# Reordering the hand-over from attention to the feed-forward stage: GpSimd takes the first row scalings

## The reference, cut to what matters

```python
x = x + cross_attention(layernorm(x), ctx_4096, Wq, bq, Wk, bk)
x = x + latent_attention(layernorm(x), ..., Wo)      # 128 heads of 8 + 64 rotary columns; out @ Wo
x = x + ffn(layernorm(x), W1, b1, W2, b2)

def _linear8bit(x, W, b):                             # ffn is two of these: 1024 -> 4096 -> 1024
    col_max = jnp.max(jnp.abs(x), axis=rows)
    outlier = col_max > 3.0
    x_in, x_out = jnp.where(outlier, 0.0, x), jnp.where(outlier, x, 0.0)
    y = quant_rows(x_in) @ quant_rows(W).T            # each row: round(a / s) * s, s = max|a| / 127
    return y + x_out @ W.T + b
```

## Time and profile before

| | |
|---|---|
| median of 3 runs | 964.59 us (961.07 to 964.97) |
| profiled execution, its own time | 964.59 us |
| its span, first to last instruction | 962.6 us |
| TensorE matmul busy | 899.3 us (93%) |
| DVE busy | 732.3 us (76%) |
| ACT busy | 607.4 us (63%) |
| GpSimd busy | 480.5 us (50%) |
| mean granted TensorE clock | 0.980 |

### The profile page before, as it was taken

The page is one execution under the profiler, slowest core; times in us unless marked ns, Lnnn a source line. Parts: engine busy times, 40 slices in busy tenths (PEclk is TensorE's granted clock), DMA queues, the critical chain, the costliest instruction groups (busy, mean ns, idle before and its releaser), DMA issues.

```text
span 962.6 us, 18936 instructions
## 1 busy us (share of the span) xinstructions
PE 899.3 (93%) x6809; PEld 821.2 (85%) x6809; DVE 732.3 (76%) x1140; ACT 607.4 (63%) x1050; POOL 480.5 (50%) x314
## 2 busy tenths in 40 slices
PE   5999999999997899999999999998779999799996
PEld 5997888888886789999999998886679999699996
DVE  6456666677446468889999998876978889899964
ACT  4424344565525478888887878782778787466652
POOL 0220000244427697767667676662176676176682
PEclk9999999999998999999999999999799999799999
DMA  7566675777663778655665655544053442224221
GB/s 276 222 221 219 266 269 213 283 303 274 259 189 100 227 241 260 188 174 176 186 195 166 194 159 172 193 164 187 15 175 104 159 165 97 88 89 176 87 88 44
DMA packets 80007, 174.81 MB, mean 182 GB/s; under 512 B 7584, under 2 KB 57536, under 8 KB 77376
## 3 DMA queue, kind: packets, MB, share of 16 engines
q1 hardware_dynamic: 79376, 173.76, 52.5%
q10 hardware_dynamic: 560, 0.09, 0.1%
HBM read 161.51 MB, written 11.53 MB: 180 GB/s over the span
## 4 chain that ended last, share of the span: by engine, by line
PE 28%; POOL 13%; issue 12%; DVE 7%; ACT 4%; DMA 1%; POOLq 0%; SPq 0%; DVEq 0%; ACTq 0%
POOL W_all L2121 8%; PE bank L51 6%; PE bank L52 6%; PE bank L53 6%; POOL W_all L1802 4%; PE bank L1268 3%; PE bank L1297 3%; PE bank L1298 2%; PE bank L1313 1%; ACT bank L1429 1%; DVE sx L1122 1%; DVE am L1496 1%; DMA ring<-in_L_attn_Wq_rope_dram 1%; POOL wl L935 1%; DVE nmax L1473 1%
## 5 line engine op out<-in xcount | busy, mean ns | idle before, releaser
L935 POOL TENSOR_TENSOR wl<-ring,wh 128x1024 fp32r<-128x1024 f32 x68 | 161.5, 2394 | 0.0
L51 PE MATMUL bank<-act_all,W_all 128*128 128x256 f32 (+1 forms) x512 | 155.6, 304 | 5.7 <-POOL W_all L1802 2.5
L51 PE MATMUL bank<-act_all,wh 128*128 128x256 f32 x512 | 144.8, 283 | 3.4 <-PEq L940 1.7
L53 PE MATMUL bank<-act_all,W_all 128*128 128x256 f32 (+1 forms) x512 | 145.3, 284 | 0.0
L52 PE MATMUL bank<-act_all,wh 128*128 128x256 f32 x512 | 144.6, 282 | 0.0
L53 PE MATMUL bank<-act_all,wl 128*128 128x256 f32 x512 | 144.0, 281 | 0.0
L457 POOL TENSOR_TENSOR xa_WT_l<-ring,xa_WT_h 128x1024 fp32r<-128x1024 f32 x16 | 43.2, 2720 | 176.8 <-ACT xa_WT_h L452 166.9
L2121 POOL TENSOR_TENSOR W_all<-rnd,W_all 128x512 fp32r<-128x512 f32 x72 | 92.3, 1293 | 59.3 <-ACT W_all L2032 59.2
L932 POOL CAST wh<-ring 128x1024 fp32r<-128x1024 f32 x68 | 68.7, 1040 | 97.7 <-PE bank L53 88.7
L1491 DVE TENSOR_TENSOR pl<-bank,ph 128x512 f16<-128x512 f32 x128 | 88.1, 688 | 32.1 <-ACT ph L1439 29.3
L51 PEld LDWEIGHTS bank<-act_all,W_all 128*128 128x128 f32 x512 | 97.6, 191 | 8.2 <-POOL W_all L1802 3.0
(11 more groups left out here) (259 smaller groups left out, 2613.5 us busy)
## 6 DMA issues: line engine op xcount, KB each, us to landing
ring<-in_ctx_dram SPq DMA_DIRECT2D x16, 2048.0 KB, 7.9
ring<-in_L_attn_Wq_rope_dram SPq DMA_DIRECT2D x32, 1024.0 KB, 6.4
ring<-in_L_ffn_W_dram SPq DMA_DIRECT2D x16, 2048.0 KB, 7.8
panel<-in_L_ffn_W_dram SPq DMA_DIRECT2D x48, 512.0 KB, 4.2
w1p<-in_L_ffn_W_dram SPq DMA_DIRECT2D x16, 512.0 KB, 3.8
ring<-in_L_xattn_Wq_dram SPq DMA_DIRECT2D x2, 2048.0 KB, 11.6
ring<-in_L_xattn_Wk_dram SPq DMA_DIRECT2D x2, 2048.0 KB, 8.4
opv<-stage SPq DMA_DIRECT2D x32, 128.0 KB, 1.7
```

Source lines behind the costliest of these rows:

```text
L51: pe.matmul(out, lh, rh, start=start, stop=False, skip_group_check=True)
L53: return pe.matmul(out, ll, rh, start=False, stop=stop, skip_group_check=True)
L935: pool.tensor_tensor(half_of(l, i), half_of(r, i), f32(half_of(h, i)), ALU.subtract).then_inc(w_lo, 1)
```

## The change

`wo_slots(1, 4, 8)` puts the last slot of `k` = 3 ahead of `attend(31)` on TensorE. On ACT, `ot_high(act, 3)` goes ahead of the two loads. On DVE, `combine(6, 0)` and `combine(6, 1)` go behind the last `low_p`. SP no longer waits for the last outputs to be loaded before it issues the load of block 0 of `W1`. The row scaling of blocks 0 and 1 of `W1` moves from ACT to GpSimd (semaphore `t_first`), as does the scaling of row tile 1 of `onat` from DVE (`ys_pool`). TensorE's first two turns of block 0 move from `y_scaled` to between the two row tiles of `y_turned`, and the turns of block 1 in `first_step` start one product earlier.

```diff
--- before.py
+++ after.py
@@ -1386,9 +1386,8 @@
                     scores_k(g, 2)
                     wo_slots(1, 2, 4)
                     scores_k(g, 3)
-                    wo_slots(1, 4, 7)
+                    wo_slots(1, 4, 8)
                     attend(g)
-                    wo_slots(1, 7, 8)
                     for k in range(4, KT):
                         for q in range(QT):
                             for h in range(2):
@@ -1461,8 +1460,8 @@
                             ot_high(act, OT_AT[g])
                     for k in (6, 7):
                         high_wo(k)
+                    ot_high(act, 3)
                     load_outputs(act, NG - 1, range(2, GROUP))
-                    ot_high(act, 3)
                     ot_high(act, 4)
 
                 def heads_vector(dve, link):
@@ -1520,14 +1519,13 @@
                         low_p(g, 2)
                         if valid(g - 1):
                             stage_outputs(dve, g - 1)
-                        if g == NG - 1:
-                            for op in range(2):
-                                combine(dve, NG // 4 - 2, op)
                         low_p(g, 3)
                         if valid(g) and g % 2 == 1 and g < NG - 1:
                             maximum_w1(LATE + g // 2)
                         if g in OT_AT and g < NG - 2:
                             ot_low(dve, OT_AT[g])
+                    for op in range(2):
+                        combine(dve, NG // 4 - 2, op)
                     stage_outputs(dve, NG - 1)
                     for op in (2, 3):
                         combine(dve, NG // 4 - 2, op)
@@ -1588,7 +1586,7 @@
                 sem(n) for n in ("y3_ready", "q1_chain", "q1_b", "q1_hi", "q1_lo"))
             ln_shift, y_act, y_dve = sem("ln_shift"), sem("y_act"), sem("y_dve")
             y_inl, y_masked, y_masked7, m_ready = (sem(n) for n in ("y_inl", "y_masked", "y_masked7", "m_ready"))
-            ys_act, ys_dve, ys_ready = (sem(n) for n in ("ys_act", "ys_dve", "ys_ready"))
+            ys_act, ys_pool, ys_ready, t_first = (sem(n) for n in ("ys_act", "ys_pool", "ys_ready", "t_first"))
             rowm = sb(ff, "rowm", [P, 2, QT])
             COLS = [slice(h * HALF, (h + 1) * HALF) for h in range(2)]
 
@@ -1883,7 +1881,6 @@
                     heads_sync(sp)
                     sp.wait_ge(w_lo, NW * 2 - 2)
                     sp.wait_ge(wo_pool, 2)
-                    sp.wait_ge(o_loaded[LAST % 2], (LAST // 2 + 1) * 4 * GROUP * 16)
                     load(sp, 0, raw(0), w1_t[0])
                     sp.wait_ge(w_lo, NW * 2)
                     sp.wait_ge(wo_pool, 3)
@@ -1928,6 +1925,11 @@
                                 last = pe.transpose(bank[4 + k // 2][:, c:c + P], onat[:, t, k * P:(k + 1) * P], ident[:, :])
                                 if t == QT - 1 and k % 2:
                                     last.then_inc(y3_ready, 1)
+                            if t == 0:
+                                pe.wait_ge(t_first, CH)
+                                pe.wait_ge(x2_done, 2)
+                                for k in range(EARLY):
+                                    turn(0, 0, k)
 
                     def masked_rows():
 
@@ -1943,16 +1945,13 @@
 
                     def y_scaled():
 
-                        pe.wait_ge(t_ready, CH)
-                        for k in range(EARLY):
-                            turn(0, 0, k)
                         pe.wait_ge(row_factor, 1)
                         for a in (6, 7):
                             pe.matmul(bank[a][:, :], zero[:, 0:P], zero[:, :], start=True, stop=False, skip_group_check=True)
                         for k in range(KT):
                             if k % 4 == 0:
                                 pe.wait_ge(ys_act, k // 4 + 1)
-                                pe.wait_ge(ys_dve, k // 4 + 1)
+                                pe.wait_ge(ys_pool, k // 4 + 1)
                             for t in range(QT):
                                 c = (k % 2) * T + t * P
                                 last = pe.transpose(bank[2 + k // 2][:, c:c + P], onat[:, t, k * P:(k + 1) * P], ident[:, :])
@@ -1981,14 +1980,14 @@
                                 turn(0, 0, 6)
                             elif k == 2:
                                 turn(0, 0, 7)
+                                pe.wait_ge(t_first, 2 * CH)
+                                turn(1, 1, 0)
                             else:
-                                if k == 3:
-                                    pe.wait_ge(t_ready, 2 * CH)
-                                turn(1, 1, k - 3)
+                                turn(1, 1, k - 2)
                             if k == KT - 3:
                                 pe.wait_ge(q1_b, 6)
                                 spread_factors(pe, 0)
-                        for k in range(KT - 3, KT):
+                        for k in (KT - 2, KT - 1):
                             turn(1, 1, k)
                         pe.wait_ge(sx_copied, 1)
 
@@ -2051,6 +2050,7 @@
                                     act.wait_ge(r_max, c * CH - (CH - 1))
                                 biased(c, b, j)
 
+                    act.sem_inc(t_ready, 2 * CH)
                     heads_scalar(act)
                     act.activation(exp_table[:, :], ident[:, 0:1], ACT.Sqrt)
 
@@ -2065,21 +2065,12 @@
                         y_row(0, h)
                     layernorm_root(act, 2, 1)
                     y_row(1, 1)
-
-                    def scale_w1(c, j):
-                        scale_rows(c, USE_W1, j, rw1[:, CH * c + j:CH * c + j + 1])
-
-                    act.wait_ge(q1_chain, 2)
-                    scale_w1(0, 0)
                     for kk in range(KT // 2 - 1):
                         act.wait_ge(y_inl, kk + 1)
                         for i in range(2):
                             k = 2 * kk + i
                             act.activation(ym[:, k, :], bank[4 + kk][:, i * T:(i + 1) * T], ACT.Copy,
                                            scale=inl1[:, k:k + 1]).then_inc(y_masked, 1)
-                    for j in range(1, CH):
-                        scale_w1(0, j)
-                    scale_w1(1, 0)
                     act.wait_ge(row_factor, 1)
                     for h in range(2):
                         act.activation(onat[:, 0, COLS[h]], onat[:, 0, COLS[h]], ACT.Copy,
@@ -2096,7 +2087,6 @@
                     for p in range(KT // 2):
                         if p < KT // 2 - 1:
                             high_y(p + 1)
-                            scale_w1(1, p + 1)
                         for k in W_AFTER[p]:
                             high(0, 0, k)
                     copy_factor(act, 0, sx1)
@@ -2121,8 +2111,18 @@
                         pool.tensor_tensor(W_l[b][:, k, :], rnd[k % 4][:, :], f32(W_h[b][:, k, :]),
                                            ALU.subtract).then_inc(b_lo, 1)
 
+                    pool.wait_ge(q1_chain, 2)
+                    for b in range(2):
+                        landed(pool, b, USE_W1)
+                        for j in range(CH):
+                            pool.tensor_scalar(raw(b)[:, j, :], raw(b)[:, j, :], rw1[:, CH * b + j:CH * b + j + 1], None,
+                                               ALU.mult).then_inc(t_first, 1)
                     pool.wait_ge(x2_ready, 2 * QT)
                     pool.memset(runmax[:, :], 0.0).then_inc(r_max, 1)
+                    pool.wait_ge(row_factor, 1)
+                    for h in range(2):
+                        pool.tensor_scalar(onat[:, 1, COLS[h]], onat[:, 1, COLS[h]], rowc[:, 2, 1:2], None,
+                                           ALU.mult).then_inc(ys_pool, 1)
                     for k in range(KT):
                         low(0, 0, k)
                     with pool.Fori(0, NW1 // 2) as i:
@@ -2237,10 +2237,6 @@
                     link(dve.tensor_tensor(rowc[:, 0, :], rowm[:, 0, :], rowm[:, 1, :], ALU.max))
                     link(dve.tensor_scalar(rowc[:, 1, :], rowc[:, 0, :], 1.0 / QMAX, TINY_SCALE, ALU.mult, ALU.max))
                     dve.reciprocal(rowc[:, 2, :], rowc[:, 1, :]).then_inc(row_factor, 1)
-                    dve.wait_ge(row_factor, 1)
-                    for h in range(2):
-                        dve.tensor_scalar(onat[:, 1, COLS[h]], onat[:, 1, COLS[h]], rowc[:, 2, 1:2], None,
-                                          ALU.mult).then_inc(ys_dve, 1)
 
                     def codes_y(p):
 
```

## The result

| | before | after |
|---|---|---|
| median | 962.94 us (961.07 to 964.97, 4 runs) | 972.19 us (971.76 to 972.57, 4 runs) |
| ratio, with its 95% interval | | 1.0096 (1.0076 to 1.0116) |
| profiled execution, its own time and span | 964.59, 962.6 | 973.34, 971.3 |
| TensorE / GpSimd busy | 899.3 / 480.5 us | 905.0 / 505.7 us |

The forecast of 964.5 and its range up to 969.0 missed: the kernel is 9.25 us slower, not unchanged.

What follows compares the result with a forecast made beforehand. TensorE, busy 93% of the span, was taken as the bound, with an idle stretch at some 665 to 715. Restart and clock -1.4, waits +2.2, turns 0, `first_step` -0.9 gave -0.1 on 964.59: 964.5 us, range 960.0 to 969.0.

Steps and rivals of the forecast that it cites:

- so I take 1.1: GpSimd's row scaling of `W1`: 1.1 us each, bounded by the cast's 1.04 and the two-input operation's 2.39.
- about 0.55: GpSimd's halves of the `onat` scaling in `first_step`: about 0.55 us each, ready no later than ACT's.
- The slow-scaling rival: Layernorm: scalings of 2.39 us make DVE's two-input operations wait, +11.8, sum +9.5, 974.1 us; chance 0.11.
- the two turns in `y_turned`: cost 0: TensorE between the row tiles: the two moved turns fit the gap and cost 0, or 0.7 without DVE's waits.
- The small loads are hurt by block 0: Rival at the end of the heads: small loads finish behind block 0, some 5 us later, 968.3 us; chance 0.11.
- The restart: TensorE's restart on the last `Wo` products: moves by 0.9 us, to 667.8; the layernorm starts 1.4 earlier.
- the combine waits behind GpSimd: DVE's second moved combine waits for GpSimd's low part of `Wo` tile 6; `stage` starts 2.0 us later, about 657.3.
- All this moves by 2.0: Store, loads and landing behind `stage`: all 2.0 us later, the small loads landing at 664.6.
- The 0.5 for those two: After TensorE's restart: two of the first six products run at the upper clock, worth 0.5 us.
- a larger one ahead of block 2: `first_step`: TensorE's wait before `step(1, 1)`, for block 2, grows to about 3.5 us.
- four signs of being wrong: 0.22 for all lines 162 and 163; a scaling over 1.3; small loads over 3 us; layernorm 3 us early.
- The one-element waits: Layernorm: DVE's one-element operations with two SBUF inputs (lines 162, 163, 2196) wait behind GpSimd's scalings, +2.2 us.

Runs made afterwards that it cites:

- e3: Changed kernel with a GpSimd tensor_copy in place of each row scaling of `W1` blocks 0 and 1 (scaling left out): 967.76 us, ratio 1.004.
- g2: Changed kernel with the constant 1.5 in place of each row's factor in GpSimd's eight scalings of `W1`: 970.87 us in one run.
- e1: Changed kernel with the row scaling of `W1` blocks 0 and 1 back on ACT and the turns where they were before: 967.51 us, ratio 1.0025.
- f6: Kernel before plus the four edits ahead of the layernorm (slot, `ot_high`, combines, early load of block 0): 966.59 us, ratio 1.0016.
- e2: Changed kernel with its two first turns of block 0 back in `y_scaled`, scalings still on GpSimd: 971.84 us, ratio 1.0076.
- f10: Changed kernel with both the first turns back in `y_scaled` and the `onat` scaling back on DVE: 968.46 us, ratio 1.0042.
- e4: Changed kernel with the row scaling of `onat` tile 1 back on DVE: 971.53 us, ratio 1.0075.
- f11: Kernel before plus slot, `ot_high` and combines edits, with SP again waiting before the load of block 0: 964.95 us, ratio 1.0006.
- f8: Kernel before plus only `ot_high(3)` ahead of ACT's two loads: 961.97 us, ratio 0.9966.
- g3: Kernel before plus the slot ahead of `attend(31)` and `ot_high(3)` ahead of the loads: 961.94 us, ratio 0.9978.
- g1: Kernel before plus `ot_high(3)` ahead of ACT's loads, all eight `W1` scalings on ACT ahead of `row_factor`, block 1's turns one product earlier: 961.01 us, ratio 0.9963.

## Why the prediction was wrong

**The step that failed: "so I take 1.1" for one row scaling.** It took 2.84, above even the end that I had called the upper bound, the two-input 2.39 of the earlier trace rows. I let the number of tensor inputs decide, as the cast's 1.04 of the earlier trace rows suggested. e3 and g2 show what decides: the copy is 1.04, the scaling with a constant 2.77. The same size failed for `onat`: halves "about 0.55", measured 1.56 (DVE 0.44 in the earlier trace rows). That put it on the path: e1 waits 1.03 and 0.48 for it, and is 0.9 above f6, less than the two intervals can tell by themselves.

**The consequence was placed on the wrong path.** The slow-scaling rival had nearly the size (2.39) and nearly the time, 974.1, but the time by luck: it let DVE's six two-input one-element operations (lines 162, 163 and 2196) pay 11.8, and in the kernel after all six took 0.16 to 0.22. Who paid most was TensorE: "the two turns in `y_turned`: cost 0" held only for 1.1 a scaling, and I never asked it at the other end of the bound. The load of block 0 landed at 671.83, four scalings take 11.34, and TensorE stood 3.69 in front of the two turns. (Less 1.52 the landing is the forecast's 670.3, but by two errors that cancel: the load was issued 2.1 earlier and took 10.0, not 7.8.) Row tile 1 was ready at 681.84, 0.8 late since DVE's line 2211 took 1.34 instead of 0.54, and was turned only at 685.11. DVE paid elsewhere than forecast, in line 2220: 4 x 0.99 less 4 x 0.17, 3.3 of busy time, 2.8 on the path. So "later by" in the table goes 3.7, 6.5, 8.3: line 2211 (0.8) and the wait for GpSimd with the turns behind it (3.3), less what the restart gained; then line 2220; then the scaling of `onat`, and turns at the lower clock (3.65 for 16, before 1.91).

e2, e4 and f10 show the turns and `onat` as gates of one list. Line 2220's share varies: from the turns of row tile 1 to `row_factor` 8.5 pass before, 11.3 in the profile after, but 9.8 in e2 and f10, 9.9 in g2 and 10.2 in e4, where GpSimd's scalings are as long. So 1.3 to 2.8 is DVE's share there, and the profile after has the dearest case. The earlier trace rows could have warned of it, since line 2154 has one tensor input and few elements and took 1.10; I read that median as one of 128x4, but it is over eleven instructions, of which the view gives that shape for one, and the best, 0.153, belongs to 128x1.

**"The small loads are hurt by block 0", 0.11.** It came true beside the other: 5.57 after the issue in the kernel after, 6.4 in f6, 2.9 in f11, 2.74 before. The cost is f6 less f11, 1.6 by the medians, not the rival's 5. In the profiled execution of e3 the loads landed 2.86 after their issue although block 0 was issued 0.71 behind them, so it does not strike every time; f6's range (964.39 to 968.61) is wider than f11's.

**The restart.** That the combine waits behind GpSimd (forecast 2 us, measured 2.61, `stage` 2.1 later against 2.0) was right. So was the direction of `ot_high`. "All this moves by 2.0" took the transport behind it as fixed, and it is not: from the store to the loads 1.72 passed instead of the 3.77 of the earlier trace rows, from the loads to their landing 5.57 instead of 2.74. In sum the landing moved by 2.6, the restart gained 0.3, not 0.9, and TensorE's gap stayed at 3.85. So the clock fell (0.56 in 668 to 669, 0.50 from 669 to 674), and all 12 products ran at the lower level (0.63 for most, before 0.39 for the last five), not two of the first six at the upper. The 0.5 for those two was my estimate: the earlier trace rows, with 0.64 in 668 to 669, gives the time of the fall before, and I held it fixed while the restart moved. No run shows that it stays: less the 1.52 it came some 1.7 earlier here (at 668.1 against 668.3, both estimated from those rows of one us). What I missed is worth more than what I had: in f8 and g3, with `ot_high` moved, the restart comes behind a gap of 0.69 and 1.41, the clock stays up, and the combines undo that (g3 to f11, 3.0).

**Right:** `stage` at 657.44 less the offset (forecast 657.3); no wait at the first turn of block 1; a larger one ahead of block 2 (2.60 here, 2.70 in g1, forecast 3.5); the slot at nothing to speak of. Three of the forecast's four signs of being wrong came: 0.22 or less for all of lines 162 and 163, a scaling over 1.3, and small loads landing over 3 us after their issue. The one-element waits exist (e3, forecast 2.2, measured 2.1). But e3, where scaling costs what I assumed, is at 967.76, not 964.5, so the size of the scaling alone does not make the forecast wrong by 7.7. The early load and `onat` on GpSimd, 1.6 and 0.9, would account for 2.5 of those 3.3.

**What adds up** (medians against 964.6): `ot_high` -2.7, slot 0, combines +3.0, early load +1.6 (966.59); scaling of `W1` on GpSimd with both gates open, which is DVE's waits less a small gain in `first_step`, +1.9 (968.46); either gate closed +3.1 or +3.4, both +3.7 (972.19). What each of the first four does in the presence of the slow scaling was not tried one by one.

## What to carry to other kernels

Where an operation has no row of its own on its new engine, ask each "cost 0" again at the dear end of its range, and then let the range reach there; a cover of 2.5 us is worth nothing behind 11 us of scaling. Work moved to an idle engine becomes one list in order: look for every consumer of that list, as undoing one gate shows nothing while the other is closed. Before work is put in front of TensorE's restart, look at how short its gap is and which operations end it: a gap that grows can cost the clock as well (here 1.41 in g3 and 2.86 in f11, and the first product behind it 0.50 and 0.79 us).

## What the runs showed of the hardware

- GpSimd's multiply by a scalar is far slower than its copy of the same 128x1024 float32: 2.84 (a factor for each row) and 2.77 (a constant) against 1.04; a half, 128x512, takes 1.56.
- DVE's small operations (one, two or eight elements wide) beside a scaling of 2.84 took at most 1.11, never the whole of it. Line 162, with two SBUF inputs, took 0.22 at 676.33 and 679.96 in the kernel after, where a scaling was well under way, and 0.95, 1.11 and 0.93 once each in e2, e4 and f10, at 677.61, 680.73 and 676.23, where one had just begun (estimated from the start of the eight and 2.84 each). One tensor input does not spare an operation: line 2220 took up to 1.11 there, line 2211 1.34, against 0.17 and 0.54 before. The combine is the other case: it started 0.06 behind GpSimd's two-input 2.39 and took 2.61, as long as the whole of it, and 0.43 before, ahead of that operation. When in a scaling such a wait falls was not tested by itself.
- Small loads issued 0.7 ahead of a 2 MB load took 5.4 (e4) to 6.4 (f6) to land in seven of eight profiles, and 2.9 in e3; without that load beside them 2.7 to 3.0 (before, f11, f8, g3, g1).
- TensorE's granted clock at the restart was still 1.00, and the first product took 0.50 us, behind gaps of 0.69 (f8), 1.41 (g3) and 2.31 (e3); it was 0.50, and the first product took 0.79 or 0.80, behind 2.86 (f11), 3.82 and 3.85 (before and after) and 4.66 (f6).
